# Accumulating transfers in place of VectorE additions on the token rows of a routed and state-space block, and a ScalarE copy of the output projection

## The reference

```
x = x + 0.5 * ffn(layernorm(x))      # 8 experts, tokens picked by a Sinkhorn gate
x = x + mixer(layernorm(x))          # projection, causal convolution, a scan with 16 states
x = x + 0.5 * ffn(layernorm(x))
```

## Time and profile before

| | |
|---|---|
| median of 3 runs | 4275.02 us (4263.61 to 4280.53) |
| the profiled execution | 4304.09 us, its span 4302.3 us |
| busy VectorE (DVE) | 3605.4 us, 84% |
| busy TensorE (PE) | 2583.4 us, 60% |
| busy ScalarE (ACT) | 1957.7 us, 46% |
| busy GpSimd (POOL) | 1373.4 us, 32% |
| `mixer`, from the first recurrence to the last addition | 538.5 to 3501.1 us of the span |

### The profile page before, as it was taken

One profiled execution on the slowest core, in us unless ns is written; L12 is line 12 of the kernel. 1 busy time (PEld: TensorE's weight loads), 2 busy tenths in 40 slices (PEclk: granted clock), 3 DMA queues, 4 the chain that ended last, 5 costly groups with the idle time before them and its releaser, 6 DMA issues. The chain is left out here.

```text
span 4302.3 us, 27806 instructions
## 1 busy us (share of the span) xinstructions
PE 2583.4 (60%) x7776; PEld 1501.1 (35%) x7776; DVE 3605.4 (84%) x3018; ACT 1957.7 (46%) x1834; POOL 1373.4 (32%) x784
## 2 busy tenths in 40 slices
PE   7501466767668566766866676685766567005553
PEld 7501232334235224422523432252343257003442
DVE  4698299999999999999999999999999946893222
ACT  4300365656555565655556555565645525001111
POOL 0000267045324703632370562246000000004665
PEclk8555788788889887988888888798889786556676
DMA  6100365557546556654755665476455545005666
GB/s 246 83 3 12 114 148 137 112 129 170 132 102 163 138 115 136 163 130 101 177 121 118 139 166 124 97 176 137 103 122 111 105 160 206 3 0 162 205 209 226
DMA packets 149396, 559.09 MB, mean 130 GB/s; under 512 B 22432, under 2 KB 74160, under 8 KB 107312
## 3 DMA queue, kind: packets, MB, share of 16 engines
q0 software_dynamic: 61440, 335.59, 37.0%
q1 hardware_dynamic: 87856, 222.40, 14.0%
HBM read 171.50 MB, written 117.46 MB: 67 GB/s over the span
## 5 line engine op out<-in xcount | busy, mean ns | idle before, releaser
L982 DVE TENSOR_TENSOR_SCAN state<-state,drive 128x2048 f32<-128x2048 f32 x512 | 2243.8, 4406 | 53.3 <-ACT state L1128 53.2
L1293 PE MATMUL ps_states<-state,ident 128*128 128x512 f32 x2048 | 1198.0, 739 | 770.3 <-DMA state<-state 700.7
L1128 ACT ACTIVATE state<-delta,neg_a 128x2048 f32<-128x2048 f32 x512 | 1022.0, 2001 | 431.8 <-DMA state<-state 272.1
L1293 PEld LDWEIGHTS ps_states<-state,ident 128*128 128x128 f32 x2048 | 470.3, 240 | 1445.0 <-DMA state<-state 813.1
L864 POOL DMA_DIRECT2D state<-state x256 | 238.3, 931 | 1448.5 <-DVE state L982 1430.3
L852 POOL DMA_INDIRECT back<-routed_rows,row_now x128 | 492.6, 3848 | 180.0 <-DMA routed_rows<-routed 98.1
L840 POOL DMA_INDIRECT picked<-normed_rows,slot_now x128 | 398.8, 3116 | 463.6 <-DVE row_now L889 229.8
L1228 PE MATMUL ps_proj<-x1t,w_in 128*128 128x512 f32 x1024 | 466.5, 595 | 11.6 <-ACT conv_in L1059 9.6
L1263 PE MATMUL ps_rows<-w_out,xc 128*128 128x256 f32 x768 | 229.3, 441 | 113.3 <-DVE resid L962 108.2
L1473 DVE COPY f_picked_t<-f_ps_turn 128x256 f32<-128x256 f32 x128 | 54.0, 424 | 278.5 <-remote 140.3
L1228 PEld LDWEIGHTS ps_proj<-x1t,w_in 128*128 128x128 f32 x1024 | 193.0, 191 | 244.9 <-issue 231.7
(11 more groups left out here) (228 smaller groups left out, 3089.8 us busy)
## 6 DMA issues: line engine op xcount, KB each, us to landing
state<-state POOLq DMA_DIRECT2D x256, 1024.0 KB, 7.0
rows_in<-in_x SPq DMA_DIRECT2D x8, 2048.0 KB, 11.7
normed_rows<-rows_in SPq DMA_DIRECT2D x8, 2048.0 KB, 7.1
expert<-in_experts SPq DMA_DIRECT2D x64, 256.0 KB
routed_rows<-routed SPq DMA_DIRECT2D x128, 128.0 KB
x<-in_x SPq DMA_DIRECT2D x8, 2048.0 KB, 12.2
x_rows<-x SPq DMA_DIRECT2D x16, 1024.0 KB, 4.0
resid<-x_rows SPq DMA_DIRECT2D x64, 256.0 KB, 7.1
```

Of the source, the lines that this page charges most:

```text
L982: nc.vector.tensor_tensor_scan(state[q % NS][:], state[q % NS][:], drive[j % 2][:], 0.0, ALU.mult, ALU.add).then_inc(state_ready, 1)
L1128: nc.scalar.activation(state[q % NS][:], delta[j % 2][:], ACT.Exp, scale=g.neg_a[:, j, n:n + 1]).then_inc(decay_ready, 1)
L1293: mm = nc.tensor.matmul(ps_sum[c][:], g.ident[:], state[q % NS][:, c * CH:(c + 1) * CH], start=(n == 1), stop=(n == N - 1))
```

## The change

- The gathered routed rows are no longer put into `back`: the indirect transfer accumulates onto `x1` in SBUF itself. VectorE's `add_routed` becomes `measure`, which only takes the statistics. `BACK` goes from 22 to 24, `ADD` stays 26.
- The result of `project_out` is copied by ScalarE into one of 4 buffers `mixed` (`copy_out`), at step 9+2r instead of 7+2r, and GpSimd adds it with an accumulating transfer onto the rows of `x1` in memory (`add_result`). The loads of `resid`, VectorE's `add_out` and SP's stores to `x2` are gone; `x2` is now a view of `x1`.

```diff
-    NS, NX, NY, NK, NRES = 6, 3, 2, 4, 4
+    NS, NX, NY, NRES = 6, 3, 2, 4
-    BACK = 22
-    ADD = BACK + NK
+    BACK = 24
+    ADD = BACK + 2
-    OUT = 7
+    OUT = 9
...
     # bring_back, GpSimd
-            pool.wait_ge(x1_added, nb * T + (t - NK + 1 if t >= NK else 0))
+                pool.wait_ge(x_in, (nb + 1) * 16)
             nc.gpsimd.indirect_dma_start(
-                out=back[t % NK][:], out_offset=None, in_=g.routed[0],
+                out=x1[:, t, :], out_offset=None, in_=g.routed[0],
                 in_offset=bass.IndirectOffsetOnAxis(ap=row_now[:, t:t + 1].bitcast(U32), axis=0)
-            ).then_inc(back_in[t % NK], 16)
+                compute_op=ALU.add).then_inc(back_in[t], 16)
...
+        def add_result(b, r):
+            if r == 0:
+                for i in range(2):
+                    pool.wait_ge(x1_stored[i], (b + 1) * 16)
+            pool.wait_ge(out_copied, b * G2 + r + 1)
+            nc.gpsimd.dma_start(out=x1_v[bass.ds(b, 1), :, 2 * r:2 * r + 2, :].rearrange("a p t d -> p (a t) d"),
+                                in_=mixed[r % NRES][:], accum_op=ALU.add).then_inc(x2_out[r % NRES], 16)
...
     # GpSimd, after the pair of an odd q
+                if not first and q in range(OUT, OUT + T, 2):
+                    add_result(b - 1, (q - OUT) // 2)
...
-        def add_routed(nb, t):
-            dve.wait_ge(back_in[t % NK], (nb * (T // NK) + t // NK + 1) * 16)
-            nc.vector.tensor_tensor(x1[:, t, :], x1[:, t, :], back[t % NK][:], ALU.add).then_inc(x1_added, 1)
+        def measure(nb, t):
+            dve.wait_ge(back_in[t], (nb + 1) * 16)
             nc.vector.bn_stats(stats[:, t, :], x1[:, t, :]).then_inc(stats_done, 1)
...
-        def add_out(b, r, last):
-            dve.wait_ge(out_done, b * G2 + r + 1)
-            nc.vector.tensor_tensor(resid[r % NRES][:]..., out_bank(r, last)[:], resid[r % NRES][:]..., ALU.add)
...
+        def copy_out(b, r, last):
+            act.wait_ge(out_done, b * G2 + r + 1)
+            act.wait_ge(x2_out[r % NRES], (b * (G2 // NRES) + r // NRES) * 16)
+            nc.scalar.copy(mixed[r % NRES][:].rearrange("p t d -> p (t d)"), out_bank(r, last)[:]).then_inc(out_copied, 1)
...
     # ScalarE, directly behind the decay of step q
+                    if not first and q in range(OUT, OUT + T, 2):
+                        copy_out(b - 1, (q - OUT) // 2, False)
                     if not last and FFN <= q <= FFN + SL:
                         read_bank(b + 1, q - FFN)
...
         def project_out(b, r, last):
             if r:
-                pe.wait_ge(out_added, b * G2 + (r - 1 if last else r))
+                pe.wait_ge(out_copied, b * G2 + (r - 1 if last else r))
```

More of the change, by code:

```diff
@@ L647, in mixer @@
     x1t = sb("x1t", [P, KD, NT])
-    resid = [sb(f"resid{i}", [P, 2, D]) for i in range(NRES)]
+    mixed = [sb(f"mixed{i}", [P, 2, D]) for i in range(NRES)]
     picked = [sb(f"picked{i}", [P, D]) for i in range(NX)]
@@ L651, in mixer @@
     routed = [sb(f"routed{i}", [P, D]) for i in range(NY)]
-    back = [sb(f"back{i}", [P, D]) for i in range(NK)]
     expert = [sb(f"expert{i}", [P, KD, D]) for i in range(2)]
@@ L678, in mixer @@
         sem(n) for n in ("res_done", "res_copied", "res_gated", "xc_done", "soft_step", "soft_done", "drive_done", "delta_done"))
-    gated, y_done, out_done, out_added = (sem(n) for n in ("gated", "y_done", "out_done", "out_added"))
+    gated, y_done, out_done, out_copied = (sem(n) for n in ("gated", "y_done", "out_done", "out_copied"))
     now_set = sem("now_set")
@@ L685, in mixer @@
     routed_out = [sem(f"routed_out{i}") for i in range(NY)]
-    back_in = [sem(f"back_in{i}") for i in range(NK)]
-    x_in, x1_added = sem("m_x_in"), sem("x1_added")
+    back_in = [sem(f"back_in{t}") for t in range(T)]
+    x_in = sem("m_x_in")
     x1_stored = [sem(f"x1_stored{i}") for i in range(2)]
@@ L768, in store_x1 @@
             for i in range(2):
-                sp.wait_ge(x1_added, nb * T + (i + 1) * TH)
+                sp.wait_ge(stats_done, nb * T + (i + 1) * TH)
                 sp.dma_start(x1_v[bass.ds(nb, 1), :, i * TH:(i + 1) * TH, :].rearrange("a p t d -> p (a t) d"),
                              x1[:, i * TH:(i + 1) * TH, :]).then_inc(x1_stored[i], 16)
[L773 to L791, removed]
         def body(b, first, last):
             if not last:
-                for i in range(NK):
-                    sp.wait_ge(back_in[i], (b + 1) * 16 * (T // NK))
-                    sp.sem_inc(g.passed_sp, 1)
+                sp.wait_ge(stats_done, (b + 1) * T)
+                sp.sem_inc(g.passed_sp, 1)
                 load_expert(b + 1, 0)
                 load_expert(b + 1, 1)
[L800 to L804, removed]
+            for s in range(0 if last else SL):
                 if s == SL - 1:
@@ L826, in _ @@
         batches(sp, body)
-        for r in range(G2):
-            store_result(NB - 1, r)
         for r in range(NRES):
@@ L878, in _ @@
         batches(pool, body)
+        for r in range(G2):
+            add_result(NB - 1, r)
     @block.vector
@@ L882, in set_now @@
         def set_now(nb):
-            for i in range(NK):
-                dve.wait_ge(back_in[i], nb * 16 * (T // NK))
+            for t in range(T):
+                dve.wait_ge(back_in[t], nb * 16)
             nc.vector.tensor_copy(slot_now[:], g.slot_token[:, bass.ds(nb, 1), :].rearrange("p a s -> p (a s)")).then_inc(now_set, 1)
@@ L957, in combine, with finish @@
                                            ).then_inc(y_done, 1)
-        def add_out(b, r, last):
-            dve.wait_ge(out_done, b * G2 + r + 1)
[L961 to L965, removed]
+        def finish(b, q):
             if q == GATE:
@@ L1011, in _ @@
         for t in range(T):
-            add_routed(0, t)
+            measure(0, t)
         aggregate(0)
@@ L1020, in _ @@
         batches(dve, body)
-        for q in range(OUT + T):
-            finish(NB - 1, q, True)
+        finish(NB - 1, GATE)
     @block.scalar
@@ L1186, in _ @@
         batches(act, body)
+        for r in range(G2):
+            copy_out(NB - 1, r, True)
     @block.tensor
```

20 lines of the change are left out of this document (7 added, 13 removed).

## The result

The changed kernel takes **4395.15 us** (median of 4 runs, 4367.79 to 4399.89) against 4277.68 for the kernel before on the same chip: a ratio of 1.028 (95% interval 1.023 to 1.032), slower. The forecast was 4358, range 4290 to 4415.

The account below looks back on a forecast made before the run. VectorE bounds most of a batch, but in steps 9 to 20 a chain through TensorE decides, which the change lengthens. 84 - 6.5 - 3 + 2 + 7 = +83 us on 4275 gives 4358, range 4290 to 4415.

Parts of the forecast that it names:

- convolution of a loop batch later: Start of a loop batch's convolution: 10.5 us later by the longer TensorE-ScalarE chain, 4.7 + 5.9 by slow pieces, 21.1 together.
- from there to the batch's end: Behind the convolution's start: VectorE's removed additions take off 6.5 us for tokens and 0.6 for the last result piece.
- six loop batches, statistics waits in: Six loop batches: +14.0 us each, +84 (49 to 119), with statistics waits of 1 us per batch besides.
- batch 0, statistics waits in: Batch 0 has no result to put out: -6.5 us, with 1 us of statistics waits besides.
- last batch: Last batch, without fills and reads: its ring starts with slack and 5.3 us of additions go, -3 us (-5 to +5).
- tail: After the last batch: an accumulating transfer of 256 KB lands instead of a plain one, +2 us (0 to +5).
- The ring: TensorE's sum and fill, ScalarE's read, decay and copy, TensorE's piece and next fill: one turn 12.8 us, TensorE idle 3.5.
- The clock: TensorE's result pieces behind waits run at the lower clock: pieces 2 and 3 +4.7 us, half of the others' 11.8, 5.9.
- The first: Rival: VectorE stays the bound throughout and its removed additions come off, giving 4194 us, faster; chance 0.09.
- The second: Rival: the ring is shorter than costed, convolution 8 us late, nearly no change, +5 us, 4280; chance 0.08.
- The third: Rival: gathers land late, VectorE waits up to 2.2 us for each of some 12 groups, 4530 us; chance 0.07.
- The fourth: Rival: GpSimd's new direct issues take a recurrence each, pairs leave 4.4 us later, 4418 us; chance 0.04.

Follow-up runs that it names:

- e3: Changed kernel with ScalarE's copy of each result piece put ahead of the decay in the same step instead of behind it: 4235.24 us, ratio 0.993 to the kernel before.
- e5: Changed kernel with ScalarE copying each piece twice inside the loop, first into a spare buffer nobody reads: 4422.61 us, ratio 1.034 to the kernel before.
- e1: Changed kernel with ScalarE's copy one step earlier, at step 8+2r, GpSimd's transfer where it was: 4162.43 us, ratio 0.974 to the kernel before.
- e2: Changed kernel with OUT = 7 instead of 9: ScalarE's copy at step 7+2r and GpSimd's addition two steps earlier: 4146.68 us, ratio 0.971 to the kernel before.
- h2: Changed kernel with the routed tokens' half taken back, so only the result's half of the change remains: 4413.7 us, ratio 1.033 to the kernel before.
- e8: Changed kernel with copy at step 7+2r, gathers from step 22 and plain result transfers, leaving out the residual addition: 4132.42 us, ratio 0.969 to the kernel before.

## Why the prediction was right, point by point

Direction, mechanism and place were right; the size was 34 us short (+83 against +117.5 between the medians). In the prediction's sum the lower bounds add up to +37.5, not +35, which changes nothing in its range. The terms, with what `mixer` shows (the sixth loop batch taken like the mean of the other five):

| term | forecast | measured |
|---|---|---|
| convolution of a loop batch later | +21.1 (15.2 to 27.0) | +22.9 |
| from there to the batch's end | -7.1 | -5.2 |
| six loop batches, statistics waits in | +90 | +106 |
| batch 0, statistics waits in | -5.5 | -6.2 |
| last batch | -3 (-5 to +5) | +4.2 |
| tail | +2 (0 to +5) | +6.9 |
| statistics waits in the prologue, and its additions | none | +5 |

- **The ring.** Turns at the full clock were forecast at 12.8 us; the first in the trace takes 12.7 (1685.38 to 1698.08). e3 and e5 confirm two of its links, e1 and e2 that it is the whole loss: without it the batch is 36 us shorter.
- **The clock.** I took pieces 2 and 3 slow and half of the other five, +10.6 us. In this batch only piece 1 was at the full clock behind its wait of 3.20, and in four of the six loop batches not even that one (2.92 to 2.94 us for its first six matmuls); pieces 4 to 7 were all slowed, wholly or in part. From a piece's start to the next sum (for piece 7 to its fill) the six took 1.5, 2.0, 1.5, 2.9, 2.8 and 1.6 us more than at the full clock: +12.3. Half was a guess between two rows, and that it came near is luck in part. The row I leaned on, a sum at full clock behind a wait of 3.36 us, had longer waits and slow sums close before it, so a wait's length alone does not tell the clock:

```profile
3444.25 3.70 PE L1293 MATMUL ps_states<-state,ident 128*128 128x512 f32 x8 [3.21 <-DMA state<-state]
3452.86 5.33 PE L1293 MATMUL ps_states<-state,ident 128*128 128x512 f32 x8 [4.91 <-DMA state<-state]
```

- **A wait that I did not name.** `combine` of the first channel group waits for the last piece (L936, 4.6 us). It lies within the +22.9, since gate, `combine` and convolution all stand behind TensorE there. But VectorE's waits in steps 8 to 20 come to 37 us, not 30.
- **Less came back.** Behind the convolution 5.2 us, not 7.1. The statistics take 1.1 (forecast as a term of its own at 1), and about 0.8 stands at `slot_now` as "issue", where VectorE now passes sixteen semaphores of the gathers; with four (before, and h2) the trace has no such row. That the number of semaphores is the cause was not tried, and with the same sixteen the row varies from batch to batch (in e2 from none to 2.10 us).
- **The last batch.** Forecast with slack and a gain; it lost 4.2, still within its bounds. The trace has 6.6 us at its gate and 2.0 at its `combine`, so the ring ends last there too, without fills or reads.
- **The prologue.** Forgotten. Ahead of the loop no recurrence hides batch 0's own gathers, and VectorE waits 1.3 to 1.6 us for most of the accumulating ones: 16 groups in 27.7 us instead of 20.7, which eats the additions saved there. It is the issue that sets this pace: GpSimd takes 1.53 us and a gap of 0.30 for each, against 0.95 and 0.30 before.
- **The tail.** The term that left its range. The +2 for a longer landing is what it costs, 4.1 us where the old stores took 2.0 at this place. What I put at nothing is the end of the part: the next one waits for GpSimd's `DRAIN`, which now begins with the last issue, some 4 us more.

The loop term is 16 of the 34 us, the last batch 7, the tail and the prologue 5 each.

**The rivals.** The first (VectorE the bound throughout) was rightly put aside for this kernel, and it is what e2 makes true; but its price of 4194 was too mild, since it kept the waits of before. The second fell with the ring's length. The third is there in small, 1.1 us a batch where it said 26. The fourth is false: the direct issues take 0.8 to 1.4 us, a recurrence 4.4:

```profile
1745.57 1.04 POOL L844 DMA_DIRECT2D state<-state  x1
1746.17 1.36 POOL L834 DMA_DIRECT2D x_rows<-mixed  x1
```

## What to carry to other kernels

When an operation moves to another engine, list what its new neighbours in that queue wait for, and whether the engine that waits for the operation is also the one that releases them: the copy itself is 0.6 us, and in the ring it cost 24 us a batch against the same copy on VectorE. Taking the decay out of the ring gave back 22, one step earlier gave back 36. Ask of each wait that the change could remove what else hangs on it, since in e2 the waits gave back 8.5 us a batch beside the work's 11.8. A half that wins and a half that loses hide in one number; run them apart.

## What the runs showed of the hardware

- A transfer of 256 KB to memory, from issue to landing, at the end of `mixer`, where no recurrence runs: 2.0 to 2.4 us issued on SP, 2.3 on GpSimd (plain, e8), 4.1 on GpSimd accumulating. Beside recurrences, behind a pair's transfer in the same queue, those of GpSimd take 7.8 us (plain, median of one batch of e8) and 8.0 to 9.1 (accumulating, one batch of the change). The Trainium skill (DMA: Bandwidth & Descriptors, "Anatomy of one DMA — SWDGE (gpsimd) path") fits a transfer issued on GpSimd with 2.0 us and the bytes by 436 GB/s, an estimate of 2.6 us here; the plain ones at the end come near it, those in the loop are far above.
- The end of a part waits for GpSimd's `DRAIN`, which was over 8.1 us behind its last accumulating issue (7.2 behind a plain one), although the transfer had landed 4.1 (2.3) us behind it.
- An accumulating gather of 128 rows into SBUF takes at least 1.53 us to issue; plain ones take 0.95, in the same place ahead of the loop before the change. Where no recurrence runs it lands in 3.8 us (median of the prologue), the plain one of the second `ffn` in 3.6. The 6.9 of the list is the median of all, most of them beside recurrences, where the plain `picked` take 5.8:

```profile
picked<-normed_rows,slot_now POOLq DMA_INDIRECT x128, 5.8
x<-routed_rows,row_now POOLq DMA_INDIRECT x128, 6.9
...
f_back<-routed_rows,f_row_now POOLq DMA_INDIRECT x128, 3.6
```

- Waits of one length left TensorE at either of its two levels. In the batch shown of the changed kernel the first six matmuls behind 3.20 us took 1.70 us once (1693.26, granted clock 1.00 up to the next sum) and 2.93 twice (1743.25 and 1757.46, granted 0.74 and 0.60); TensorE had run for 14.5, 11.5 and 11.0 us without a gap before these. In its last batch four waits of 2.56 us gave 2.93, 1.70, 1.71 and 2.93. Waits of 1.31 us left it at the full level in every loop batch of e3. What decides between the two is not shown. The Trainium skill (TensorE: Matmul & The Clock Gate, Part 1) has the lower level as the default, which only activity lifts; e2, with TensorE busy without a gap, shows 1.00 in the window above and agrees.
